# Memory attention: the order of softmax, output product and rotation in a one-core megakernel

## The reference

```
q, k, v = split(layernorm(x) @ w_qkv)          # 16 heads of 64
qr, kr  = rope(q), rope(k)                      # t * cos + rot(t) * sin
for each segment of 32 positions:               # 32 of them, one after the other
    p     = softmax(mask(qr_s @ kr_s.T / 8)) @ v_s
    sq,sk = elu(q_s) + 1, elu(k_s) + 1
    out   = beta * (sq @ mem) / (sq @ z + 1e-6) + (1 - beta) * p
    prev  = (sk @ mem) / (sk @ z)
    mem  += sk.T @ (v_s - prev);  z += sum(sk)
x = x + concat(out) @ w_out
```

## Time and profile before

| | |
|---|---|
| median of 3 runs | 2843.09 us (2839.88 to 2843.68) |
| profiled execution | 2834.01 us, span 2832.2 us |
| busy over the span | PE 2060.4 us (73%), DVE 1949.3 (69%), ACT 1397.4 (49%), POOL 1134.8 (40%) |
| memory attention | about 317 to 1121 us, in it PE 705.87 us, DVE 626.43, ACT 347.88, POOL 385.07 |
| granted clock of PE, mean over the span | 0.799 of 2.4 GHz; 0.92 in the memory attention |

### The profile page before, as it was taken

The page is one execution under the profiler, slowest core; times in us unless marked ns, Lnnn a source line. Parts: engine busy times, 40 slices in busy tenths (PEclk is TensorE's granted clock), DMA queues, the critical chain, the costliest instruction groups (busy, mean ns, idle before and its releaser), DMA issues. The chain is left out here.

```text
span 2832.2 us, 85356 instructions
## 1 busy us (share of the span) xinstructions
PE 2060.4 (73%) x34174; PEld 1672.8 (59%) x34174; DVE 1949.3 (69%) x4625; ACT 1397.4 (49%) x2280; POOL 1134.8 (40%) x929
## 2 busy tenths in 40 slices
PE   3678489999999996567568994765666555557895
PEld 2567378888888885456446993552222233336795
DVE  4678678887777776667664444598999777764443
ACT  1545344444444442435445551368999644435452
POOL 3655455444444443545555561002000222216464
PEclk7789699999999997679868995685555678868998
DMA  4123200000000000122331222003333000021224
GB/s 110 44 85 99 82 3 0 0 0 0 0 0 0 0 0 3 33 74 75 99 97 57 81 67 70 0 0 60 59 59 58 2 2 0 0 74 39 77 77 118
DMA packets 103650, 120.78 MB, mean 43 GB/s; under 512 B 23224, under 2 KB 85288, under 8 KB 102848
## 3 DMA queue, kind: packets, MB, share of 16 engines
q1 hardware_dynamic: 82544, 80.39, 11.7%
q0 software_dynamic: 18176, 37.79, 4.0%
q10 hardware_dynamic: 2768, 0.55, 0.2%
HBM read 60.00 MB, written 46.20 MB: 37 GB/s over the span
## 5 line engine op out<-in xcount | busy, mean ns | idle before, releaser
L2451 DVE CUSTOM_DVE_ANT_0 be_logs<-be_joint,be_logs 128x1024 f32<-128x1024 f32 x256 | 293.3, 1224 | 10.2 <-ACT be_logs L2434 9.2
L2434 ACT ACTIVATE be_logs<-be_joint,b_tiny 128x1024 f32<-128x1024 f32 x256 | 283.9, 1115 | 19.5 <-PE be_joint L2419 11.9
L2419 PE MATMUL be_joint<-be_parts_k,be_parts_q 64*128 64x512 f32 x512 | 202.4, 789 | 108.8 <-DVE be_sums L2451 91.3
L2657 POOL TENSOR_TENSOR bw_kT<-b_knT,b_head_of 128x768 f32<-128x768 f32 x40 | 58.5, 1497 | 440.2 <-POOLq L63 287.3
L446 POOL DMA_INDIRECT d_pairs<-s_y_tile,s_x_tiles x156 | 179.1, 1148 | 130.8 <-DVE s_y_tile L1388 105.1
L446 POOL DMA_INDIRECT d_pairs<-g_y_tile,g_x_tiles x156 | 160.6, 1029 | 141.5 <-ACT g_y_tile L883 100.9
L2419 PEld LDWEIGHTS be_joint<-be_parts_k,be_parts_q 64*128 64x128 f32 x512 | 73.7, 285 | 237.3 <-DVE be_sums L2451 216.5
L1736 POOL TENSOR_TENSOR m_roped_q<-m_raw_q,kg_xn 128x512 f32<-128x512 f32 x64 | 82.7, 1292 | 310.7 <-ACT m_raw_q L1667 310.7
L1218 PE MATMUL s_ps_y<-s_down,s_a_tile 128*128 x1248 | 151.7, 275 | 0.0
L1388 DVE TENSOR_SCALAR s_y_tile<-s_ps_y,s_x_tiles 128x128 f32<-128x128 f32 x156 | 47.5, 346 | 150.5 <-PE s_ps_y L1218 86.0
L1498 PE MATMUL m_front<-m_xnT,kg_xn 128*128 128x128 f32 x1024 | 146.7, 287 | 1.0 <-ACT m_xnT L1655 0.6
(11 more groups left out here) (498 smaller groups left out, 6370.0 us busy)
## 6 DMA issues: line engine op xcount, KB each, us to landing
g_x_tiles<-d_rows SPq DMA_DIRECT2D x78, 132.0 KB
s_x_tiles<-d_rows SPq DMA_DIRECT2D x78, 132.0 KB
d_rows<-d_rows SPq DMA_DIRECT2D x32, 132.0 KB
s_down<-L_ffn_We SPq DMA_DIRECT2D x16, 256.0 KB, 5.0
be_parts_q<-be_high_q SPq DMA_DIRECT2D x64, 64.0 KB, 2.3
be_parts_q<-b_soft_q SPq DMA_DIRECT2D x64, 64.0 KB, 2.3
be_parts_k<-be_high_k SPq DMA_DIRECT2D x60, 64.0 KB, 2.3
be_parts_k<-b_soft_k SPq DMA_DIRECT2D x60, 64.0 KB, 2.3
```

Of the source, the lines that this page charges most:

```text
L2419: last = nc.tensor.matmul(joint_ps[k % DEPTH][:, a, :], parts[b % 2][0][rows, i * P:(i + 1) * P], parts[b % 2][1][rows, half * 512:(half + ...
L2434: nc.scalar.activation(logs[k % DEPTH][:, :, :], joint_ps[k % DEPTH][:, :, :], ACT.Ln, bias=A.tiny[:, :]).then_inc(s.log_ready, 1)
L2451: nc.vector.tensor_tensor_reduce(out=flat, in0=joint_ps[k % DEPTH][:, :, :].rearrange("p a j -> p (a j)"), in1=flat, scale=1.0, scalar=0.0 ...
```

## The change

The edit moves instructions on four engines and splits one. On PE the scores of the next tile stand before the output product, and the first additions before the first half of k's fill. The recall for k waits for X's addition only ahead of its second half. On DVE `back_x` of the tile before stands behind `softmax_1`, o's first half straight behind u, the sum of the exponentials between o's halves, the inverse after the turned q, and the scale and the transpose between the two memory halves; `split_x` stands behind the memory, the statistics of tile w+2 at the head of the tile. On ACT the first half of k is copied ahead of q's exp. On POOL k's cosines are two halves, with 1/sqrt(var) between them. Names of instructions and shapes stay, except for those halves.

```diff
             def recall_k(w):
                 wait(pe, s.mem_done, 2 * w)
-                wait(pe, s.x_done, w)
                 wait_alone(pe, s.phi_ready, at(w, 2, 2), s.passed)
                 recall(phi_kT, 0)
+                wait_alone(pe, s.x_done, w, s.passed)
                 recall(phi_kT, 1)
...
+            def copy_front(f, k, half):
                 full, copied = ((s.q_full, s.q_copied), (s.k_full, s.k_copied))[k]
-                wait(act, s.cos_done, at(f, 3, 2 * k) - 1)
...
+            def front(f):
+                copy_front(f, 0, 0)
+                copy_front(f, 0, 1)
+                front_relu(f, 0)
+                copy_front(f, 1, 0)
+                front_exp(f, 0)
+                copy_front(f, 1, 1)
+                front_relu(f, 1)
+                front_exp(f, 1)
...
+            def cosines(f, k, half):
+                pool.wait_ge((s.q_copied, s.k_copied)[k], at(f, 2, half + 1))
+                if half == 0:
+                    wait(pool, s.scores_full, f)
+                part = slice(4 * half, 4 * half + 4)
+                nc.gpsimd.tensor_tensor(roped[k][:, part, :], raw[k][:, part, :], wide(cos).broadcast_to([P, 4, P]), ALU.mult).then_inc(s.cos_done, 1)
+
+            def rope_sum(f, k):
+                pool.wait_ge(s.cos_done, at(f, 4, 2 * k + 2))
                 pool.wait_ge(s.rot_done, at(f, 4, 2 * k + 2))
                 nc.gpsimd.tensor_tensor(roped[k][:, :, :], roped[k][:, :, :], turned[k][:, :, :], ALU.add).then_inc(s.rope_done, 1)
...
             def tile(w):
                 more = not (isinstance(w, int) and w == TILES - 1)
                 norm = more and not (isinstance(w, int) and w == TILES - 2)
+                if norm:
+                    norm_1(w + 2)
                 softmax_1(w)
+                if not (isinstance(w, int) and w == 0):
+                    back_x(w - 1)
                 back_u(w, 0)
                 back_u(w, 1)
-                softmax_2(w)
                 back_o(w, 0)
-                if more:
-                    split_x(w + 1)
+                softmax_sum(w)
                 back_o(w, 1)
                 if more:
                     front_rope(w + 1, 0)
+                softmax_inverse(w)
                 back_mem(w, 0)
-                if norm:
-                    norm_1(w + 2)
+                softmax_scale(w)
                 back_mem(w, 1)
+                if more:
+                    split_x(w + 1)
+                    front_phi(w + 1, 0)
                 if norm:
                     norm_2(w + 2)
                 if more:
-                    front_phi(w + 1, 0)
                     front_rope(w + 1, 1)
-                if more:
                     front_phi(w + 1, 1)
-                back_x(w)
```

More of the change, by code:

```diff
@@ L1603, in project @@
                 for k in range(PAIRS):
[L1604 removed]
+                    last = nc.tensor.matmul(out_ps, oT[:, k, :], w_out[:, k, :], start=(k == 0), stop=(k == PAIRS - 1))
                 last.then_inc(s.back_full, 1)
@@ L1660, in split_x, with front_relu, front_exp @@
                 nc.scalar.copy(x_high[:, :], xnT[:, :]).then_inc(s.x_split, 1)
[L1662 removed]
+            def copy_front(f, k, half):
                 full, copied = ((s.q_full, s.q_copied), (s.k_full, s.k_copied))[k]
[L1664 to L1672 removed]
+                if half == 0:
+                    wait(act, s.cos_done, at(f, 4, 2 * k - 2))
+                act.wait_ge(full, at(f, 4, 2 * half + 1))
+                nc.scalar.copy(raw[k][:, 4 * half:4 * half + 4, :], front_ps[2 * half][:, :].rearrange("p (k t) -> p k t", t=P)).then_inc(copied, 1)
+            def front_relu(f, k):
+                act.wait_ge((s.q_copied, s.k_copied)[k], at(f, 2, 2))
+                wait(act, s.phi_ready, at(f, 2, k - 1))
+                nc.scalar.activation(relu[k][:, :], raw[k][:, :, :].rearrange("p k t -> p (k t)"), ACT.Relu)
+            def front_exp(f, k):
+                nc.scalar.activation(expo[k][:, :], raw[k][:, :, :].rearrange("p k t -> p (k t)"), ACT.Exp).then_inc(s.elu_ready, 1)
+            def front(f):
[7 more added lines that the diff above has]
+                front_exp(f, 1)
             def copy_v(f):
@@ L1712, in _ @@
             split_x(0)
-            front(0, 0)
-            front(0, 1)
+            front(0)
             copy_v(0)
@@ L1727, in rstd_of @@
                 nc.gpsimd.tensor_tensor(rstd[:, :], var[:, :], c.minus_half[:, 0:1], ALU.pow).then_inc(s.ln_rstd, 1)
-            def rope(f, k):
-                copied = (s.q_copied, s.k_copied)[k]
-                for part in ((slice(0, 4), slice(4, 8)) if k == 0 else (slice(0, 8),)):
-                    pool.wait_ge(copied, at(f, 2, part.stop // 4))
-                    if part.start == 0:
-                        wait(pool, s.scores_full, f)
-                    count = part.stop - part.start
-                    nc.gpsimd.tensor_tensor(roped[k][:, part, :], raw[k][:, part, :], wide(cos).broadcast_to([P, count, P]), ALU.mult).then_inc(s.cos_done, 1)
-                pool.wait_ge(s.cos_done, at(f, 3, 2 + k))
+            def cosines(f, k, half):
+                pool.wait_ge((s.q_copied, s.k_copied)[k], at(f, 2, half + 1))
+                if half == 0:
+                    wait(pool, s.scores_full, f)
[3 more added lines that the diff above has]
+                pool.wait_ge(s.cos_done, at(f, 4, 2 * k + 2))
                 pool.wait_ge(s.rot_done, at(f, 4, 2 * k + 2))
@@ L1744, in tile @@
                 if more:
-                    rope(w + 1, 0)
+                    cosines(w + 1, 0, 0)
+                    cosines(w + 1, 0, 1)
+                    rope_sum(w + 1, 0)
+                    cosines(w + 1, 1, 0)
                 if norm:
@@ L1755, in _ @@
                 rstd_of(f)
-            rope(0, 0)
-            rope(0, 1)
+            for k in range(2):
+                cosines(0, k, 0)
+                cosines(0, k, 1)
+                rope_sum(0, k)
             in_tiles(pool, tile)
@@ L1923, in _ @@
             in_tiles(dve, tile)
+            back_x(TILES - 1)
 B_HEADS, B_DH = 8, 16
```

23 lines of the change are left out of this document (12 added, 11 removed).

## The result

The changed kernel took 2895.74 us (median of 4 runs, 2892.78 to 2897.28) beside 2842.62 us for the kernel before: a ratio of 1.0187, interval 1.0169 to 1.0205. That is 53 us slower; I had forecast 102 us slower, 2945 us with a range of 2860 to 2995. The sign and the mechanism were right, the size was about twice too large; of the cases with a time of their own, rival B (2908 us) lies nearest. The profiled execution took 2892.78 us, 58.8 us more than that of before.

What follows compares the result with a forecast made beforehand. One dependency closing the memory attention loop, not PE, was taken as the bound, at 23.9 us a tile. The steps summed to 27.2, 3.3 more; over 31 passages 102 us: 2834.0 to 2936, plus 9 for the median, 2945 us (2860 to 2995).

Steps and rivals of the forecast that it cites:

- rival B: Memory attention: one hold less, or PE's first 13 us at full clock; period 26.0 us, 2908 us; chance 16%.
- likeliest case: Memory attention loop: product on the path, scale held twice, sum behind phi; period 27.2 us, 2945 us; chance 50%.
- the signs that I had named: Scores 27 us apart, PE waiting over 2, srec 1.3 or more, scaling 1.8, split 0.4 or more, sum 3.1.
- The product on the path: PE: output product behind the scores adds 1.9 us, moving the recall for q from 5.8 to 7.7 us.
- rival C: PE: slow clock takes the output product as well, 1.45 us more; period 28.65 us, 2990 us; chance 13%.
- o and the memory's first half: DVE: o done at about 12.5 us, additions follow the turned q at once, first memory half done at 15.5.
- The scale held twice: DVE: srec product held by q's sum, scaling by k's first cosines; 2.4 us lost, bounds 0 and 3.6.
- rival A: DVE/POOL: scale slips past POOL, only k's phi holds the sum; period 24.65 us, 2866 us; chance 10%.
- Split, phi, turned k: DVE: behind the second memory half come split of x, q's phi, xn and turned k, done at 23.75 us.
- the gain of the halved cosines: POOL: halves save 1.8 us only if cosines are last; the turned k is, by 2.7 us, so gain zero.
- phi ahead of the sum: DVE/POOL: k's phi starts first, POOL's sum ends 2.20 us behind it at 27.05, scores at 27.2 us.
- The covers: Free moves: X's addition done at 3.8 us, wanted at 4.9; were DVE 1.1 late, PE pays one for one.

Runs made afterwards that it cites:

- experiment 5: Kernel before with only the scores ahead of the output product, X's addition behind softmax_1 and its wait between the recall's halves: ratio 1.0312 to the kernel before.
- experiment 4: Changed kernel with the scale's two products replaced by one-input reductions of the same shapes, exponentials not scaled: ratio 1.014 to the kernel before.
- experiment 1: Changed kernel with the softmax's sum, inverse, scale and transpose back in one piece between u and o: ratio 1.0357 to the kernel before.
- experiment 3: Changed kernel with k's cosines as one POOL instruction behind 1/sqrt(var): ratio 1.0368 to the kernel before.
- experiment 8: Changed kernel with k's phi on DVE waiting until POOL's sum for k is done: ratio 1.0087 to the kernel before.
- experiment 7: Changed kernel with the normalised x (xn) behind the turned k, all else as changed: ratio 1.0188 to the kernel before.
- experiment 2: Changed kernel with the output product ahead of the scores again, all else as changed: ratio 1.0244 to the kernel before.

## Why the prediction was right, and what it sized wrongly

The prediction had the period at 27.2 us; a tile with a quick product took 24.9 and one with a slow product 26.4, 25.6 on average. 1.6 us a tile over 31 passages is the 50 us by which I missed. The measured time lies in the stated range, but the range is wide, 17 to 152 us of loss, so the mechanism has to be read from the rows. The likeliest case had the holds right and the front of the tile too long. B came nearest in time (26.0 us a tile): one of its two conditions, a front at the full clock, held in every second tile.

Of the signs that I had named, srec at 1.3 us or more, the scaling near 1.8 and a sum for k of 3.1 us came (1.52, 1.71, 3.19). The split of x was at 0.36 and not 0.4, the scores came 24.9 to 26.4 us apart and not 27, and PE waited over 2 us for POOL only in every second tile.

1. **The product on the path: right in kind (experiment 5), wrong in size.** This is the term that was mis-sized. I put the recall for q at 7.7 us and it came at 5.8 (639.98 to 645.75), and at 7.25 in the slow tile. I had added 1.9 us to the 5.77 of a tile that already paid for the slow stretch in its recall and transposes, and left both where they were. In fact the slow stretch moved. By the groups above, a tile has 2.75 us of product (74.2 / 27) where 1.95 was expected, +0.80; recall for k and transposes fall from 3.52 us (52.5 / 29 + 49.7 / 29) to 2.61 (40.9 / 27 + 29.5 / 27), -0.91; and the gap of 0.48 us (14.0 / 29) ahead of the recall is gone. Together the front grows by 1.3 us and not 1.9. And the front of the tile I started from was itself 0.4 us above the average: its recall and transposes took 3.91 us (1.94 and 1.97) where the mean is 3.52. Timeline of before, PE, the tile of the earlier trace rows:

```profile
664.74 1.94 PE L1554 MATMUL m_back<-m_mem,m_phi_kT 64*32 64x65 f32 x128 [0.47 <-issue]
666.61 1.97 PE L1538 MATMUL m_front<-ident,m_phi_kT 128*128 128x128 f32 x8
```

That makes 1.0 of the 1.6 us, and the small differences of points 3 and 4 another 0.4. Counted tile by tile, the recall for q starts 6.55 us after the scores on average (28 tiles from 432.61 us: 5.8 in 13, 7.1 to 7.7 in 15), which is 1.15 less than my 7.7, and the rest of a tile takes 19.1 us (24.9 less 5.8) where I had 19.5. In the quick tiles all 1.9 us are missing, because there the product ran at 2.4 GHz and so did all that follows it. I had the two prices in hand (the 4.59 us of a tile with a quick front, and 3.40 for a slow product) and made one of them into part of rival B and the other into rival C. They are one thing: where there was a slow stretch between the scores and the recall for q, it lay in one place or in the other, and never in both.

2. **o and the memory's first half: right.** With the turned q's second fill at 11.4 (650.30 + 1.06), the first addition into the memory ends at 13.5; by my lengths from the fill it should have been 13.6.

3. **The scale held twice: right.** srec ended with q's sum, the scaling behind k's first cosines. From the fill's end to the end of the second memory half I had 7.5 us; it took 7.2 (658.52 less 651.36). That rival A failed is shown by the rows; that these are holds is shown by experiment 4.

4. **Split, phi, turned k: right in length, wrong in one rule.** From the second memory half to the turned k I had 2.95 us; it took 2.9 (658.52 to 661.40). The split took 0.36 in place of 0.28. But my sentence that only DVE operations with both inputs in SBUF are held is wrong: xn, a tensor_scalar with one matrix, took 1.29 us under the cosines (experiments 1 and 4). In the changed kernel itself it met nothing (0.34), so this cost the forecast nothing. And the gain of the halved cosines was zero only against a trace in which they met nothing: experiment 3.

5. **phi ahead of the sum: right.** 3.3 us from the end of the turned k to the end of the sum, as in the prediction; experiment 8 takes 0.8 of it away, and in experiment 7 phi stayed ahead of the sum even with xn between it and the turned k.

**The covers.** The addition into X cost nothing, as said, but its cover was the product (experiment 2). PE stood 1.66 us at the answers for the second memory half, as the prediction had said it would, and that cost nothing by itself, since PE stood again for POOL.

**What stays open.** Why the slow stretch falls into the product in every second tile here, and in all or most of them in experiments 3 and 5, is not explained. In the changed kernel the length of the wait at the scores goes with it: from 432 us on, 14 waits of 2.50 us or a little more were each followed by a slow product, and 13 waits of 1.10 to 1.24 by a quick one (a single one of 0.83 by a slow one). But the wait does not decide alone. In experiment 5, 26 waits of 2.73 to 2.75 us were followed by 21 slow products and 5 quick ones (2.05 us at 783.40), and in experiment 8 eight waits of 1.67 to 1.69 us by 6 slow and 2 quick. And the short wait is itself made by the clock: in the tile of the slow product the v products run slow as well (0.80 us for the first, at 687.47, where it is 0.50 at 660.70, with a granted clock of 0.50 from 687 to 689), so that PE comes later to the next scores and stands there 1.18 us instead of 2.50. That the gap ahead of the recall for k went away with the product's move is seen and was not tested.

## What to carry to other kernels

When work is moved behind a wait, look in the trace whether the slow stretch moves too, as it did here. Then add the moved work at one clock and take the slow price away from where it was, or the same microsecond is counted twice.

Before each reorder write down which small VectorE operations with SBUF inputs will fall under which GpSimd operation, since 16 elements can cost 1.5 us. Write down also what each edit that you cost at nothing is hidden behind, since the cover may be another edit of the same change.

A loop closed by several near-equal chains gives back most of any one saving. In the kernel before, waits of 0.8 and 1.6 us a tile were taken away, and 0.2% was the most that came of it. In the changed kernel, where POOL's sum came 1.2 to 2.5 us after PE was ready, the same 0.8 us brought its full 1.0% (experiment 8).

## What the runs showed of the hardware

POOL's sum began at 700.96 by its row and still waited for a phi that began at 701.00, with xn directly ahead of phi on DVE (experiment 7). In that kernel two operations of DVE without a gap between them acted as one turn, tile after tile (the sum's median is 3.46 us); it is one place in one kernel, not a rule. Short POOL operations are held the same way: rstd, one element wide, took 1.52 us under q's phi instead of 0.55 (experiment 4).

xn under the cosines went from 0.34 to 1.29 us, though it reads one matrix and two columns of scalars. The Trainium skill, "SBUF — State Buffer", section Who interferes with whom, counts tensor_scalar among the operations that can enter a mode with both ports and can then contend with GpSimd; these rows agree that it can be held, and do not show by which mode. The reductions of experiment 4, with one input, kept 0.16 and 0.69 us under the same sum and cosines.

A granted clock of 0.50 followed a wait of about 1 us at the scores as well as one of 2.5 us. What changed with the order was above all what stood in the slow stretch: before, recall and transposes were slow in 21 of 28 tiles, and after, the product in 15 of 28, where it goes from 2.05 to 3.46 us. The mean clock of the stretch 400 to 1090 us hardly moved, 0.95 before and 0.93 after.
